# An eight-core transformer layer: the softmax norm of a query block moved behind the next block's first exponentials

## The reference

```python
x = x + attn_a(layernorm(x))          # phase-rotated cumulative sums, then Wo
x = x + layernorm(x) @ sign(weight).T
x = x + attn_b(layernorm(x))          # below
x = x + layernorm(x) @ sign(weight).T

def attn_b(x):                        # H = 16, D = 64
    Q, K, V = x @ Wq.T + bq, x @ Wk.T + bk, x @ Wv.T + bv
    wei = einsum('bhqd,bhkd->bhqk', Q, K) / 8
    att = softmax(where(causal, wei, -inf))
    return einsum('bhqk,bhkd->bhqd', att, V) @ Wo.T + bo
```

## Time and profile before

| | |
|---|---|
| median of the runs | 1676.53 us (1676.28 to 1676.78, 2 runs) |
| profiled execution, span of its slowest core (core 2) | 1680.1 us |
| spans of the eight cores in it | 1652.6 to 1680.1 us |
| mean granted TensorE clock, core 2 | 0.773 |
| PE busy | 1013.5 us, 60% |
| DVE busy | 835.7 us, 50% |
| ACT busy | 641.3 us, 38% |
| POOL busy | 57.0 us, 3% |
| attention stage (attn_b) up to its output projection | about 800 to 1485 us |

### The profile page before, as it was taken

How to read it: one execution, slowest core, us unless ns; L and a number is a source line. 1 busy time by engine, 2 the same in 40 slices (tenths; PEclk the granted TensorE clock), 3 DMA queues, 4 the chain that set the end, 5 groups by cost and what they waited for, 6 DMA issues and landing times.

```text
span 1680.1 us, 16252 instructions; the slowest of 8 cores (1652.6 to 1680.1 us)
## 1 busy us (share of the span) xinstructions
PE 1013.5 (60%) x5031; PEld 430.6 (26%) x5088; DVE 835.7 (50%) x1072; ACT 641.3 (38%) x747; POOL 57.0 (3%) x69
## 2 busy tenths in 40 slices
PE   0355343442311961960787878787878788778458
PEld 0111111110100420420433333333333334233123
DVE  1658889888898347446432323222323222225553
ACT  2434333343220042042055555555555546721400
POOL 1000000000000100001000000000000000000000
PEclk9766656765665975975897878787878888789679
DMA  9003212311001300100302020202020200022024
GB/s 252 0 1 38 30 15 31 37 13 13 0 4 9 32 7 13 32 7 8 31 1 20 1 20 1 20 1 20 1 20 1 20 1 1 1 25 26 0 75 176
DMA packets 73156, 42.03 MB, mean 25 GB/s; under 512 B 67696, under 2 KB 67696, under 8 KB 71024
## 3 DMA queue, kind: packets, MB, share of 16 engines
q0 software_dynamic: 66592, 16.78, 11.2%
q1 hardware_dynamic: 6480, 24.21, 4.4%
HBM read 47.28 MB, written 10.49 MB: 34 GB/s over the span
## 4 chain that ended last, share of the span: by engine, by line
PE 47%; DVE 29%; ACT 10%; DMA 6%; issue 5%; DVEq 1%; POOL 1%; SPq 1%; ACTq 0%; POOLq 0%
PE PC L655 7%; PE PC L724 5%; PE PRB L799 5%; PE POB L900 4%; PE PRB L845 4%; PE PRB L822 4%; PE POB L904 4%; DVE POOLBF L404 3%; DVE LNT L409 3%; PE PD L528 2%; PE PC L923 2%; DVE POOLBF L598 2%; DVE POOLBF L580 2%; DVE POOLBF L573 2%; DVE POOLBF L592 2%
## 5 line engine op out<-in xcount | busy, mean ns | idle before, releaser
L968 ACT ACTIVATE POOLBF<-PC 128x1024 bf16<-128x1024 f32 x128 | 131.1, 1024 | 160.7 <-PE PC L928 80.3
L860 DVE CAST POOLBF<-PRB 128x128 bf16<-128x128 f32 x128 | 37.7, 294 | 179.8 <-PE PRB L851 178.4
L900 PE MATMUL POB<-POOLBF 128*65 128x512 bf16 (+1 forms) x320 | 122.9, 388 | 0.8 <-DVE PF L1024 0.8
L904 PE MATMUL POB<-POOLBF 128*65 128x512 bf16 (+1 forms) x320 | 117.8, 383 | 0.0
L265 ACT ACTIVATE LNT<-XT 128x2048 bf16<-128x2048 f32 x16 | 30.6, 1910 | 226.7 <-PE PC L655 155.2
L968 ACT ACTIVATE POOLBF<-PD 128x1024 bf16<-128x1024 f32 x96 | 98.3, 1024 | 14.7 <-PE POB L904 0.9
L528 PE MATMUL PD<-LNT,WSB 128*128 128x512 bf16 x125 | 38.6, 474 | 93.5 <-ACT POOLBF L536 93.1
L655 PE MATMUL PC<-BIG,WSA 128*128 128x512 bf16 x251 | 60.3, 399 | 46.7 <-DVE BIG L610 40.8
L314 PE MATMUL POB<-LNT,ONESB 128*1 128x512 bf16 x128 | 41.5, 483 | 68.9 <-DVE LNT L260 43.7
L1007 PE MATMUL POB<-PF,ONESRB 1*64 1x512 bf16 x64 | 28.5, 445 | 84.5 <-DVE PF L1003 55.0
L528 PE MATMUL PD<-LNT,WSA 128*128 128x512 bf16 x125 | 38.4, 471 | 65.6 <-ACT POOLBF L536 65.4
(11 more groups left out here) (157 smaller groups left out, 2089.4 us busy)
## 6 DMA issues: line engine op xcount, KB each, us to landing
XT<-xT SPq DMA_DIRECT2D x8, 1024.0 KB, 17.6
yT<-XT SPq DMA_DIRECT2D x8, 1024.0 KB, 4.9
BIG<-wts POOLq DMA_DIRECT2D x8, 256.0 KB, 7.3
wsgn<-BIG SPq DMA_DIRECT2D x8, 256.0 KB, 2.4
WSA<-wsgn SPq DMA_DIRECT2D x8, 256.0 KB, 3.0
WSB<-wsgn SPq DMA_DIRECT2D x8, 256.0 KB, 3.7
WSA<-wk POOLq DMA_DIRECT2D x4, 256.0 KB, 4.5
WSA<-wv POOLq DMA_DIRECT2D x4, 256.0 KB, 7.5
```

The lines of the kernel that those rows point to most:

```text
L900: t.matmul(PO0[0:65, o:o + N], VSB[:, kt * 130:kt * 130 + 65], ep[:, 0:N], start=(kt == 0), stop=(kt == nkt - 1))
L904: return t.matmul(PO1[0:65, o:o + N], VSB[:, kt * 130 + 65:kt * 130 + 130], ep[:, 512:512 + N], start=(kt == 0), stop=(kt == nkt - 1))
L968: return s.activation(ep[:, 0:1024], ps[:, 0:1024], AF.Exp)
```

## The change

The three lines that carry out a pending norm move, within the round of the `kc` loop, from behind the scores to behind the exponentials. Everything else stays: the same instructions, the same waits on other steps.

```diff
                         ts_ = b.op("tensor", mm_s, wait=w, sem="T", inc=1)
                         exp_toks.append([ts_, None])
-                      if pending_norm[0] is not None:
-                          norm_done = pending_norm[0]()
-                          pending_norm[0] = None
                       if pending:
                           pending.pop(0)()
                       while avq and avq[0] <= kc - 1:
...
                         exp_toks[kt] = te
                         avq.append(kt)
+                      if pending_norm[0] is not None:
+                          norm_done = pending_norm[0]()
+                          pending_norm[0] = None
                     while avq:
                         plan_av(avq.pop(0))
                     prev_qs_exp = exp_toks[-1]
```

## The result

| | before | after |
|---|---|---|
| median of all runs | 1680.9 us (10 runs) | 1720.5 us (12 runs) |
| ratio after to before | | 1.0236 (95% interval 1.0226 to 1.0246) |
| profiled execution, span of the slowest core | 1680.1 us | 1718.0 us |
| profiled execution, mean over the eight cores' spans | 1661.8 us | 1714.2 us |

The move costs 39.5 us, 2.4%.

The account below looks back on a forecast made before the run. TensorE's order of work, with its stalls and clock, was taken to set the pace. Terms 13.0 + 13.7 + 8.0 + 3.4 = 38.1 us, less 3 for the clock, gave +35: 1711.5 us, range 1698 to 1729 (8 in 10).

Parts of the forecast that it names:

- The chain: Norm's Ln, broadcasts and second scores queued behind exponentials 0 and 1: broadcast two late by 2.66 us.
- the thin margin: VectorE's first copy, behind the unit's eviction, was to end 0.3 us ahead of what ScalarE allows for broadcast one.
- Q and K boundaries: 14 block boundaries with a Q or K unit: 0.93 us lost at each, 13.0 us in all.
- the last three of the last pair: Three boundaries with no unit, so nothing is given back: 2.66 us each, 8.0 us in all.
- the first of the last pair: Boundary from seventh pair to last, no matmul unit: broadcast two later by 3.41 us, all counted, 3.4 us.
- The pair's first block: Six other boundaries between pairs: later norm hidden under TensorE's wait for weights, 0 us; without this cover 20 us.
- The clock: Low TensorE clock behind the stall at 21 boundaries: little changed, -0.15 us each, -3 us, bounds -13 to +17.
- V boundaries: Seven boundaries with a V unit of 0.71 us: 1.95 us lost at each, 13.7 us in all.
- the clock would stay up: Rival: unit fills the stall's start, clock no longer falls at 21 boundaries, about 2.2 us back each; 1668.5 us, chance 0.05.
- The early exponentials: Rival: exponentials starting earlier let TensorE catch up behind V units, the 13.7 us fall away; 1698 us, chance 0.08.
- The memset: Rival: V tile's memset, now beside the POOL issues, delays weight DMAs at pair boundaries; +10.8 us, 1722 us, chance 0.06.
- The late copy: Rival: VectorE copy behind the eviction late by 1.3 us at 7 to 14 boundaries; plus 9 to 18, 1725 us, chance 0.07.

Follow-up runs that it names:

- x_act: Kernel after, with only the norm's ScalarE part (Ln, Exp) back ahead of exponentials 0 and 1; four runs 1683.3, 1688.7, 1743.4 and 1787.2 us, no ratio.
- w_before: Kernel before, with idle matmuls in its stalls around the broadcasts at Q, K, V and last-pair boundaries; ratio to before 0.9685, 1632.0 us.
- w_after: Kernel after, with idle matmuls in its stalls around the broadcasts at Q, K, V and last-pair boundaries; ratio to before 0.9886, 1663.0 us.
- m_first: Kernel before, with only the memset of the next V tile moved ahead of the norm at boundaries between pairs; ratio to before 1.0001.
- x_pe: Kernel after, with Ln and Exp back ahead of the exponentials and the first VectorE copy ahead of the unit's eviction; TensorE order kept; ratio to before 0.9860.

## Why the prediction was right, and where only its sum was

The prediction gave 1711.5 us, +35 us; measured are 1720.5 us against 1680.9, +39.5.

*The chain.* Broadcast one was put at +4.45 and came at +4.40, broadcast two at +6.54 and came at +6.49, the second scores at +6.84 to +7.1 and came at +7.02. That ScalarE sets broadcast one with VectorE 0.3 us ahead holds at 29 of the 31 boundaries, and x_act shows what the thin margin meant. With the clock held up, Q and K boundaries cost 0.86 and 0.80 us (forecast 0.93), V 1.91 (1.95) and the last three of the last pair 2.5 to 2.65 (2.66). At the first of the last pair broadcast two moved by 3.58 us (forecast 3.41). All these terms hold.

*The pair's first block, costed at nothing.* Over all cores its mean is unchanged, 13.66 to 13.72 us (-0.04 with idle work), but as a balance of two things, not because the wait covers the move everywhere. The last weight load is issued 1.6 us behind the pair's first scores in both kernels. It lands on the mean at +9.5 us on cores 2 and 3 of before and at +8.0 to +8.3 on the other six. On most of those the cover was thin: no first Q unit of after starts ahead of +8.31, where before had some at +7.7, and without the two late cores of each execution (4 and 5 in after, +9.0 and +9.3) the block grows from 13.2 to 13.6 us. On the late cores it shrinks from 15.2 to 14.0. On the slowest core it goes from 15.27 to 13.66, 9.7 us gained. The prediction read core 2 alone. There the first Q unit stood 9.96 us behind the pair's first scores (917.04 - 907.08), while in after's slowest core, not a late one, it stands at +8.31 (919.37 - 911.06) without waiting. I costed the cover from one core's wait, and core 2 was a late one.

*The clock, the term that was mis-sized.* The prediction held that the loss behind the stall stays at about 2.2 us a boundary and took -3 us in all, within -13 to +17. It is 1.8 us before and 2.9 us after at Q and K boundaries, 2.0 and 2.1 at V (from w_before and w_after): over 14 and 7 boundaries +17 us on the mean of cores. The reasoning was that the loss would fall on equally dense work. What the rows show: before, the K unit right behind broadcast two had 3.39 us of slow work, and the scores behind it took 0.54 us, between the 0.60 of the low and the 0.39 of the high clock: the clock was coming back (949.28). In after the scores (0.60, 0.63) and the whole unit behind them (3.60) and the first weighted sums (0.63 at 956.33) are slow. Over these boundaries the clock was low for 3.4 us before and 6.7 us after. The prediction said that where the clock returns can't be read from rows; windows over the boundaries of before show it. At V boundaries the clock was low for 6.2 us on the mean before, so there was little to add. Why the low clock lasts longer behind the longer stall no run shows. I gave the upper bound and chose the wrong side of it. On core 2, which had long slow stretches at its Q blocks already (19.3 us, against 18.3 over all cores), the surplus is smaller.

*The sum.* On the slowest cores: Q and K +23.1 us where 13.0 was forecast, V +13.0 (13.7), last pair +12.2 (11.4), the pair's first -9.7 (0), and no -3. The clock's 10 us too much at Q and K and the 9.7 us gained at the pairs' starts cancel. So the time was right by the chain, and within 5 us by that cancellation, which is luck. On the mean of cores the move costs 52 us, and there the forecast of 35 would have been 17 us short: the clock's +17 in place of -3, less 3 us by which the chain's terms were high.

*The rivals.* That the clock would stay up is refuted: it falls at every Q, K and V boundary of after. With work in the stall, in w_after, it stays up and gives 57 us back. The early exponentials give nothing: the V blocks lose 2.0 us, 1.9 of it the chain. The memset delays no issue; the Trainium skill's rule on this, that only certain modes of copy, cast and tensor_scalar, or two SBUF inputs against a GpSimd read, shut GpSimd out (SBUF — State Buffer, "Who interferes with whom"), agrees with m_first, where issues beside the memset took 0.89 and 0.90 us. The late copy appeared at two of the 31 boundaries, both with a K unit and the same two on all cores: broadcast one waited for VectorE there and came at +4.58 us, late by 0.2 us and not by 1.3. Three more in core 3 have it at +4.62 to +4.69, but behind a later Ln.

## What to carry to other kernels

When a step spans several in-order engines, ask for each queue what is put ahead of it; here filling TensorE's stall with a unit was worth a gain (x_pe), and queueing the same step behind two exponentials on ScalarE and an eviction on VectorE turned it into a loss. At Q and K boundaries either queue alone holds broadcast one back by nearly as much as both; at V boundaries and in the last pair it is ScalarE's alone. Take the clock apart from the chain by running idle matmuls in the stalls of both kernels: it is a cheap test, but the idle work must end before the step is due, and it showed that 49 us of before and 57 us of after were the clock's. And cost a cover (a DMA wait) from all cores, not from the slowest one's profile, and read from windows how long the low clock lasts behind a stall before moving the stall.

## What the runs showed of the hardware that was not expected

- At Q and K boundaries a TensorE stall of some 4.6 us, with two short lone matmuls in it, brings 6.8 us at the low clock each time, from the end of the stall on, and costs 2.9 us. One of some 3.6 us brings 4.2 us of it on the mean and costs 1.8, but not the same each time: at 11 of the 56 Q boundaries of before the clock did not fall at all (second scores at +6.0 instead of up to +7.9), at others it stayed low for up to 6.8 us. Idle matmuls in the stalls, which compute nothing, bring the pair's mean granted clock from 0.83 to 0.92 and after's time from 1720 to 1663 us.
- The kernel before is spread over its cores (1652.6 to 1680.1 us) although all do the same work; after is not (1711.6 to 1718.0 us). Between cores 2 and 5 of before the attention stage differs by 23 us: 13 in the six first blocks (15.27 against 13.03 us) and 10 in the seven Q blocks (19.29 against 17.83), where the low clock lasted 6.4 us on core 2 and 2.9 on core 5. In w_before, with the clock up, the Q blocks are alike on all cores (16.56 to 16.60 us) and only the first blocks still differ, 15.1 us on cores 4 and 5 against 12.8 to 13.3 on the others, with the last weight load landing at +9.5 against +7.8 to +8.2. So a good half of the spread is the weights' arrival and the rest the clock. Why two neighbouring cores get their weights late, and why the first blocks of such cores are shorter in after (13.9 and 14.0 us), stays open.
